# A later residual add, maxima 26 heads ahead and joined value products in a fused cross attention and FP4 feed-forward kernel

## The reference

```python
def xattn(Q, K, V):                        # per item, 16 heads, d = 16
    scores = einsum('bhqd,bhkd->bhqk', q, k) * 0.25
    attn = softmax(scores, axis=-1)
    return einsum('bhqk,bhkd->bhqd', attn, v)
def fp4_linear(x, w):                      # blocks of 16 scaled by max|.|/6, rounded to E2M1
    return einsum('bsk,nk->bsn', quant(x), quant(w))
x = x + xattn(layernorm(x), ctx, ctx)      # K = V = ctx
n = layernorm(x)
h = silu(fp4_linear(n, w_gate)) * fp4_linear(n, w_up)      # 256 -> 704
x = x + fp4_linear(h, w_down)                              # 704 -> 256
```

## Time and profile before

| | us |
|---|---|
| median of three runs | 639.03 |
| the profiled execution | 640.17 |
| its span, first to last instruction | 638.4 |
| PE busy in the span | 562.2 (88%) |
| DVE busy | 518.7 (81%) |
| ACT busy | 357.2 (56%) |
| POOL busy | 324.4 (51%) |

### The profile page before, as it was taken

How to read it: one execution, slowest core, us unless ns; L and a number is a source line. 1 busy time by engine, 2 the same in 40 slices (tenths; PEclk the granted TensorE clock), 3 DMA queues, 4 the chain that set the end, 5 groups by cost and what they waited for, 6 DMA issues and landing times.

```text
span 638.4 us, 13006 instructions
## 1 busy us (share of the span) xinstructions
PE 562.2 (88%) x3588; PEld 338.5 (53%) x3588; DVE 518.7 (81%) x1171; ACT 357.2 (56%) x656; POOL 324.4 (51%) x386
## 2 busy tenths in 40 slices
PE   2489999999999999999887999999999999999995
PEld 1135545544455455454555666656656656656664
DVE  1498888888888888887678899899898898898864
ACT  2227877777777777776734454454454454453441
POOL 3343334334434433432266766766767767667640
PEclk9999999999999999999998999999999999999998
DMA  7834444444434444310000000000000000000000
GB/s 234 185 100 135 135 133 125 114 116 131 132 105 122 115 113 126 99 52 3 2 0 1 17 18 8 16 16 8 16 16 8 16 16 8 16 16 8 17 17 25
DMA packets 43795, 40.58 MB, mean 64 GB/s; under 512 B 4728, under 2 KB 43512, under 8 KB 43768
## 3 DMA queue, kind: packets, MB, share of 16 engines
q1 hardware_dynamic: 43768, 40.26, 22.3%
HBM read 10.55 MB, written 4.19 MB: 23 GB/s over the span
## 4 chain that ended last, share of the span: by engine, by line
DVE 42%; PE 24%; issue 19%; ACT 4%; POOL 4%; DVEq 3%; DMA 2%; SPq 2%; POOLq 0%; ACTq 0%
DVE QS L725 8%; DVE MF L543 6%; PE MX L845 5%; PE SC L831 5%; PE PV L863 5%; DVE hmax L735 4%; DVE hinv L607 3%; PE T L772 3%; DVE KS L753 3%; ACT QS L489 2%; POOL KN L363 2%; DVE hinv L611 2%; DVE onrm L599 2%; PE SC L943 2%; DVE stats L551 2%
## 5 line engine op out<-in xcount | busy, mean ns | idle before, releaser
L543 DVE TENSOR_REDUCE MF<-MX 128x2 f32<-128x512 f32 x256 | 171.1, 686 | 41.7 <-PE MX L845 37.7
L456 ACT ACTIVATE P<-SC 128x512 f32<-128x512 f32 x256 | 148.4, 597 | 56.1 <-PE SC L831 54.8
L845 PE MATMUL MX<-KS,QS 96*128 96x256 bf16 x512 | 104.0, 288 | 8.1 <-DMA QS<-QP 3.6
L943 PE MATMUL SC<-KS,QS 128*128 128x256 f32 x384 | 92.7, 392 | 17.2 <-ACT QS L505 17.2
L831 PE MATMUL SC<-QS,KS 98*128 98x256 bf16 x512 | 99.8, 277 | 1.4 <-DMA QS<-MT 0.6
L943 PEld LDWEIGHTS SC<-KS,QS 128*128 128x128 f32 x384 | 71.6, 193 | 42.3 <-ACT QS L505 33.6
L863 PE MATMUL PV<-P,VA 128*32 128x256 f32 x1024 | 81.6, 391 | 0.0
L407 POOL TENSOR_TENSOR QS<-QS 128x256 f32<-128x256 f32 (+1 forms) x47 | 48.4, 1029 | 53.4 <-ACT QS L500 35.8
L831 PEld LDWEIGHTS SC<-QS,KS 98*128 98x128 bf16 x512 | 39.0, 98 | 59.6 <-ACT P L456 36.3
L845 PEld LDWEIGHTS MX<-KS,QS 96*128 96x128 bf16 x512 | 46.5, 100 | 32.4 <-DVE MF L543 22.7
L409 POOL TENSOR_TENSOR QS<-QS 128x256 f32<-128x256 f32 (+1 forms) x47 | 49.8, 1060 | 3.7
(11 more groups left out here) (107 smaller groups left out, 1016.2 us busy)
## 6 DMA issues: line engine op xcount, KB each, us to landing
KS<-KP SPq DMA_DIRECT2D x96, 128.0 KB, 2.4
QS<-QP SPq DMA_DIRECT2D x96, 128.0 KB, 2.4
X<-in_x SPq DMA_DIRECT2D x16, 256.0 KB, 2.8
C<-in_ctx SPq DMA_DIRECT2D x16, 256.0 KB, 3.0
out<-KS SPq DMA_DIRECT2D x16, 128.0 KB, 1.7
out<-QS SPq DMA_DIRECT2D x16, 128.0 KB, 1.7
W<-in_L_ffn_w_down SPq DMA_DIRECT2D x1, 704.0 KB, 8.0
W<-in_L_ffn_w_gate SPq DMA_DIRECT2D x1, 640.0 KB, 4.9
```

The costliest lines, as they stand in the source:

```text
L456: nc.scalar.activation(P[g % 2][:, j, :, :], SC[h % 3][:, :, :], ACT.Exp, scale=0.25).then_inc(exp_done, 1)
L543: nc.vector.tensor_reduce(MF[st.slot(off, 2)][:, :, h:h + 1], MX[h % 2][:, :, :], AX.X, ALU.max, negate=True).then_inc(mx_done, 1)
L845: last = nc.tensor.matmul(MX[h % 2][:, q, :], QS[r][0:PROD, h, q * 128:(q + 1) * 128], KS[r][0:PROD, h, :], start=True, stop=True)
L943: last = nc.tensor.matmul(DP, HT[r][:, c, :], WDT[:, c, :], start=(c == 0), stop=(c == NT - 1))
```

## The change

It has five edits. The names of items are relative to step t.

- POOL's additions to X1 move from the end of the step, where they served item t-1, to right behind KN (L363), where they serve item t-2; the steps of POOL are unrolled differently, and there is one more, t = 17, for the last item.
- `AHEAD` goes from 24 to 26: max_scores and maximum run 26 heads ahead of scores. The last maximum of item t+1 is then taken in slot (1,1) and not in (1,3).
- DVE's maxima_high and maxima_low move from (2,0) to (1,2), maxima_out from (2,3) to (2,0); PE's maxima from (2,2) to (2,0). PE's outputs(0) moves from (2,0) to (2,2) and waits for maxima_out now, outputs(1) from (3,0) to (3,1). DVE's denominators and output move from (2,1) to (2,3) and from (3,1) to (3,2).
- K's second rest moves from (1,2) to (1,1); Q's flip from (1,3) to (1,2), its first rest from (2,2) to (2,1); ACT takes the first part of Q out at (1,3), not (2,0).
- The halves of the value products, at j = 1 and j = 3, are both issued at j = 2, one behind the other.

```diff
@@ -30,7 +30,7 @@
 ROWS = PROD + 2
 RING = 4
 CONSTS = 8
-AHEAD = 24
+AHEAD = 26
 LEAD = 3
 
 
@@ -362,6 +362,14 @@
                     for q in range(QT):
                         nc.gpsimd.tensor_scalar(KN[:, q, :, :, :], by_parity(C[rc][:, q, :]), 1.0, 0.0,
                                                 ALU.mult, ALU.add).then_inc(kn_ready, 1)
+                if st.has(-2):
+                    for q in range(QT):
+
+                        xt = X1[:, bass.ds(st.item(-2) * (QT * D) + q * D, D)]
+                        pool.wait_ge(o_norm, st.times(-2, QT, q + 1))
+                        nc.gpsimd.tensor_tensor(xt, xt, onrm[q][:, :, :].rearrange("p h d -> p (h d)"),
+                                                ALU.add).then_inc(x1_ready, 1)
+                if st.has(LEAD):
                     pool.wait_ge(stats_seq, st.times(LEAD, 4, 4))
                     gate(pool)
                     nc.gpsimd.tensor_scalar(ve[r][:, :], mv[:, :, 1], EPS, None, ALU.add).then_inc(ve_ready, 1)
@@ -393,14 +401,6 @@
                     pool.wait_ge(w_seq, st.times(LEAD, 4, 4))
                     gate(pool)
                     nc.gpsimd.tensor_tensor(blocks(ws), blocks(ws), each(winv[:, :]), ALU.mult).then_inc(w_scaled, 1)
-                if st.has(-1):
-                    for q in range(QT):
-
-                        xt = X1[:, bass.ds(st.item(-1) * (QT * D) + q * D, D)]
-                        pool.wait_ge(o_norm, st.times(-1, QT, q + 1))
-                        nc.gpsimd.tensor_tensor(xt, xt, onrm[q][:, :, :].rearrange("p h d -> p (h d)"),
-                                                ALU.add).then_inc(x1_ready, 1)
-
             def grid(z, c, sem_, wait_sem, st, off):
 
                 pool.wait_ge(wait_sem, st.times(off, 1, 1))
@@ -424,13 +424,14 @@
                     pool.wait_ge(fve_ready, st.times(3, 1, 1))
                     nc.gpsimd.tensor_tensor(frstd[r][:, :], fve[r][:, :], mhalf[:, 0:1], ALU.pow).then_inc(frstd_ready, 1)
 
-            attention_steps(pool, attention_step)
+            steps(pool, attention_step, -LEAD, 2, 2, RING, B - 1, B)
 
             for t in (-3, -2):
                 ffn_step(Step(t, TILES, 2))
             attention_step(Step(B - 1, B, RING))
             ffn_step(Step(-1, TILES, 2))
             attention_step(Step(B, B, RING))
+            attention_step(Step(B + 1, B, RING))
             pool.wait_ge(sc_ready, B * H + 1)
             for r in range(2):
                 nc.gpsimd.memset(HQ[r][:, FI:], 0.0).then_inc(zeroed, 1)
@@ -477,7 +478,7 @@
                                 part_out(KP[st.slot(LEAD, 2)], TA, n, k_tr, k_out, st)
                         if (g, j) == (0, 3) and st.has(-1):
                             evacuate(st, -1, 1)
-                        for n, at in enumerate(((2, 0), (2, 2), (3, 1))):
+                        for n, at in enumerate(((1, 3), (2, 2), (3, 1))):
                             if (g, j) == at and st.has(LEAD):
                                 part_out(QP[st.slot(LEAD, 2)], TB, n, q_tr, q_out, st)
                         if (g, j) == (2, 3) and st.has(0):
@@ -656,16 +657,15 @@
                             normalise(st, 0)
                         if (g, j) == (1, 0) and st.has(LEAD):
                             normalise(st, 1)
+                        if (g, j) == (1, 2) and st.has(1):
+                            maxima_high(st)
+                            maxima_low(st)
                         if (g, j) == (2, 0) and st.has(1):
-                            maxima_high(st)
-                        if (g, j) == (2, 0) and st.has(1):
-                            maxima_low(st)
-                        if (g, j) == (2, 1) and st.has(-1):
+                            maxima_out(st)
+                        if (g, j) == (2, 3) and st.has(-1):
                             denominators(st, 0)
                             output(st, 0)
-                        if (g, j) == (2, 3) and st.has(1):
-                            maxima_out(st)
-                        if (g, j) == (3, 1) and st.has(-1):
+                        if (g, j) == (3, 2) and st.has(-1):
                             denominators(st, 1)
                             output(st, 1)
                         if (g, j) == (1, 3) and st.has(LEAD - 1):
@@ -799,8 +799,7 @@
             def maxima(st):
                 pe.wait_ge(m_parts, st.times(1, 1, 1))
                 pe.wait_ge(k_out, st.times(LEAD, 3, 3) if st.has(LEAD) else 3 * B)
-                if st.has(-1):
-                    pe.wait_ge(o_norm, st.times(-1, 2, 1))
+                pe.wait_ge(o_norm, st.times(-1, 2))
                 for q in range(QT):
                     last = nc.tensor.transpose(TA16[0:2 * H, q * 128:(q + 1) * 128],
                                                MP[st.slot(1, 2)][:, q, :, :].rearrange("p a h -> p (a h)"), identb[:, :])
@@ -811,7 +810,7 @@
 
                 pe.wait_ge(k_out, st.times(LEAD, 3, 3) if st.has(LEAD) else 3 * B)
                 pe.wait_ge(o_norm, st.times(-1, 2, q))
-                if q == 1 and st.has(1):
+                if q == 0 and st.has(1):
                     pe.wait_ge(mt_ready, st.times(1, 1, 1))
                 for g in range(NG):
                     last = nc.tensor.transpose(TA[:, g * 128:(g + 1) * 128],
@@ -881,23 +880,22 @@
                     for j in range(HG):
                         scores(st, g, j)
                         max_scores(st, g, j)
-                        for n, at in enumerate(((0, 0), (0, 3), (1, 2))):
+                        for n, at in enumerate(((0, 0), (0, 3), (1, 1))):
                             if (g, j) == at and st.has(LEAD):
                                 keys(st, n)
-                        for n, at in enumerate(((1, 3), (2, 2), (3, 0))):
+                        for n, at in enumerate(((1, 2), (2, 1), (3, 0))):
                             if (g, j) == at and st.has(LEAD):
                                 queries(st, n)
-                        if (g, j) == (2, 0) and st.has(-1):
+                        if (g, j) == (2, 0) and st.has(1):
+                            maxima(st)
+                        if (g, j) == (2, 2) and st.has(-1):
                             outputs(st, 0)
-                        if (g, j) == (2, 2) and st.has(1):
-                            maxima(st)
-                        if (g, j) == (3, 0) and st.has(-1):
+                        if (g, j) == (3, 1) and st.has(-1):
                             outputs(st, 1)
                         if st.first == B - 1 and HG * g + j < LOTS:
                             transpose_weights(HG * g + j)
-                        if j == 1:
+                        if j == 2:
                             values(st, g, 0)
-                        if j == 3:
                             values(st, g, 1)
 
             def inner(st, a, m):
```

## The result

The changed kernel takes 646.41 us (645.60 to 647.24, 4 runs) against 638.82 for the kernel before (638.53 to 639.84, 4 runs): a ratio of 1.0107, 95% interval 1.0077 to 1.0136. It is 1.1% slower; forecast was 626.0. The profiled execution took 647.24 us, its span 645.4.

The account below looks back on a forecast made before the run. Attention steps were taken as bound by onrm, POOL's additions, KN and PE's flip. Savings of 11.0 - 0.15 + 0.5 + 1.2 + 1.2 - 0.8 = 13.0 us gave 626.0 against the median, range 618 to 634 for 8 in 10.

Parts of the forecast that it names:

- The wait for KN costs 1.16 a step and goes: Attention steps: PE's flip waits for KN behind POOL's additions, worth 1.16 us a step; moving the additions removes it.
- The step's layout: Steps 2 to 12 laid out slot by slot from the first score product: 17.51 to 16.5 us each, 11.0 in all.
- In the last step two more additions come in a row ... nothing: POOL, last step: two more additions, 1.5 us, cost nothing because POOL has to wait for DVE there anyway.
- Steps 13 to 15: 2.4 less: End of the attention phase: step 13 takes 1.2 us less, steps 14 and 15 together 1.2 less.
- AHEAD: +0.8, step 0 0.5 shorter, step 1 0.15 longer: Start: two more maxima ahead of step 0 add 0.8 us; step 0 takes 0.5 less, step 1 0.15 more.
- The joined lump: PE, both value halves at j = 2: 1.00 us from its start to the next score product, where halves apart cost 1.32 more.
- Rival C: Joined halves are no cheaper, holding PE for 1.32 us: steps of 17.4 to 17.5, 637 to 639 us; chance 0.08.
- A: The moved waits don't show, DVE fills the holes better: steps of 15.4 to 16.0, 615 to 620 us; chance 0.20.
- B: PE's flip waits for the second onrm in KN's place: 4.4 us less gained, 630.5 us; chance 0.15.
- D: Q's stack lands late at (1,2), holding PE's max product of head 0: slower, 642 to 665 us; chance 0.07.
- DVE's idle time at (2,3): Sign in the profile after: DVE idle 1 us and more at (2,3), waiting for max products behind the value lump.
- the first score product 0.8 later: Sign in the profile after: the first score product comes about 0.8 us later than 48.63.

Follow-up runs that it names:

- e2: Kernel before with only POOL's additions moved behind KN and one step later, item 14's ahead of feed-forward step -1: 629.56 us, ratio 0.9823.
- e3: As e1, with head 15's scores in bank 1 in place of bank 0: 633.50 us, ratio 0.9888 to the kernel before.
- e1: Changed kernel with POOL's additions for item 14 ahead of feed-forward step -1, not behind it: 641.05 us, ratio 1.0023 to the kernel before.
- e5: As e2, but item 14's additions behind POOL's feed-forward step -1, as in the changed kernel: 633.96 us, ratio 0.9882 to the kernel before.
- e4: As e1, with the halves of the value products back at j = 1 and j = 3: 630.70 us, ratio 0.9853 to the kernel before.
- e9: As e4, with the last of four groups of value products joined at (3,3): 624.55 us, ratio 0.9779 to the kernel before.
- e12: As e9, with the group of g = 2 joined at (2,1) as well: 633.25 us, ratio 0.9864 to the kernel before.
- e10: As e2, with the last of four groups of value products joined at (3,3): 629.97 us, ratio 0.9850 to the kernel before.

## Why the prediction was wrong

- *The wait for KN costs 1.16 a step and goes.* Right: e2 gained 1.06 a step with this edit alone.
- *The step's layout.* "SC(3,3) 16.07, max product 16.29, next step 16.51" is the step that failed. SC(0,0) can't start before exp(3,3) has read bank 0; 1.17 lies between them and not 0.44. The rest of the layout stood: without this wait the step is 16.49 (e3), and the stall ahead of outputs(1) (forecast 0.8, found 0.51) and at K's second rest were seen. The wait cost 0.69 in each step, 7.6 us over steps 2 to 12, where 11.0 were forecast and 3.6 found.
- *"In the last step two more additions come in a row ... nothing".* This is the other failed step. I priced the additions' own 1.5 us against POOL's idle time and didn't ask who waits for them. DVE's `output` does, through the single `onrm[q]`, and a feed-forward step stood ahead of them: 3.3 us more of waiting and 6.2 in the trace with what came behind it, 5.4 between the medians of the changed kernel and e1; e5 brought the stall back.
- *Steps 13 to 15: 2.4 less.* Step 13 alone, forecast 1.2 shorter, is 0.9 longer, and step 15 is 2.1 longer with the clock that fell in it. The bank wait accounts for 1.2 of what lies between flip 12 and the last value products (e1 to e3). With the halves apart 3.5 is regained (e4), and with it the clock in step 15. How much of the rest is the clock's and how much that of PE's waits, no run separates.
- *AHEAD: +0.8, step 0 0.5 shorter, step 1 0.15 longer.* The first score product came at 48.80, only 0.2 later; steps 0 and 1 took 17.14 and 17.01, 1.0 and 0.7 longer than before. But the time to step 2's flip ranges from 80.6 to 83.8 in kernels that share this order's start (e9, e1), so AHEAD's share stays open.
- *The joined lump.* 1.01 from its start to the next score product, as taken. But four of them were to save up to 0.92 a step, and the step with them is 16.49 (e3, the bank mended) against 16.55 with the halves apart (e4). Their real price was no term of my sum: joining took away work that stood between a wait and what is awaited. I had looked for new waits at the slots that moved, and missed those that a moved half had covered. Rival C, with lumps of 1.32 and steps of 17.4 to 17.5, came nearer than I did to the 17.18 found, but by a cause that did not occur, and its 637 to 639 lacks the tail.
- *Rivals A, B and D.* None came. The flip never waited for onrm, and for DVE's QN once, 0.2; PE never stood at (1,2) for Q's stack. The additions never met the QN pair, whose two halves took 0.50 each as before.
- *A reading.* Line 725 took 0.42 us five times in 32, not once.

Of the signs that I had named, the end of the wait for KN, DVE's idle time at (2,3) (1.16 before the maximum at 249.95), the stall at outputs(1) and the value products as x16 in 1.07 came; the step of 16.3 to 16.7 and the first score product 0.8 later did not.

Together, cut at the first score products as the forecast was: up to step 2 the changed kernel is 1.8 us later (forecast 0.45), steps 2 to 12 are 3.6 shorter (11.0), from there to the last value products it takes 2.7 more (2.4 less), and behind them 6.2 more (nothing). Against the 13.0 less forecast it fell short by 1.3, 7.4, 5.1 and 6.2.

## What to carry to other kernels

Before you move or join work on an in-order engine, list for each piece which wait follows it: a piece that fills a wait is nearly free where it stands, and its length shows elsewhere. A list of waits doesn't show those that a piece is covering (e12); it takes the timeline. Look at buffer reuse across the loop's edge, since a bank index such as h % 3 over 16 heads makes neighbours of the last and the first. When a consumer moves a step later, follow its buffer back to the producer in the last, irregular steps as well, where other work has got into the queue ahead of it.

## What the runs showed of the hardware

The price of an idle PE was more than its idle time, in some places. After the wait of 4.3 us at the end of the attention phase the granted clock was 0.57 over the next 4 us, and after the waits at the start of step 15 it was 0.80 and 0.63 over 3 us each. In e1 and the kernel before, where PE waited 1.0 us at the first of these places, it stayed at 1.00 there. But the length of a wait doesn't decide it alone: e2 has no wait over 1.0 us there and its clock was 0.57 from 308 to 312, at the start of its feed-forward products. In step 15, PE's wait for the weight copies was 1.5 us in the changed kernel and in e10, and in e10 the clock stayed at 1.00 up to the last value products; in e9 it was 1.8, and the clock behind it 0.58 from 288 to 292. What else decides these runs don't show.

Of the joined value products, the second half added 0.43 us to the first's 0.64 at full clock (x16 in 1.07 in the changed kernel), as in the earlier trace rows. In the changed kernel's step 15, where the clock was 0.80 from 302 to 305, the same x16 took 1.66 (at 303.49).
